# Two TensorE groups moved within the slot of a pipelined attention and feed-forward stack

## The reference

```
def attn_layer(x, Wqkv, qs, ksc, Wo):
    q, k, v = split(x @ Wqkv)                  # 16 heads of 64
    q = l2norm(q) * qs ;  k = l2norm(k) * ksc
    q = q * cos * scale + rotate_half(q) * sin * scale
    k = k * cos / scale + rotate_half(k) * sin / scale
    out = local_attention(q, k, v)             # windows of 32, each sees itself and the one before
    return out @ Wo

def ffn_layer(x, g, bln, W1, b1, W2, b2):
    xn = (x - mean) / sqrt(var + 1e-5) * g + bln
    a, gate = split(xn @ W1 + b1)
    return a * gelu(gate) @ W2 + b2

for i in range(6):
    x = attn_layer(shift_tokens(x), ...) + x
    x = ffn_layer(shift_tokens(x), ...) + x
```

## Time and profile before

| | |
|---|---|
| median of 3 runs | 4420.13 us (4412.47 to 4425.89) |
| the profiled execution | 4411.89 us |
| its span, first to last instruction | 4410.1 us |
| mean granted TensorE clock | 0.966 of full speed |
| TensorE busy | 93% of the span |
| VectorE, ScalarE, GpSimd busy | 79%, 70%, 41% |
| first and last Q projection of the first stack | 393.3 and 2174.8 us |
| first and last Q projection of the second stack | 2553.7 and 4335.5 us |

### The profile page before, as it was taken

One profiled execution on the slowest core, in us unless ns is written; L12 is line 12 of the kernel. 1 busy time (PEld: TensorE's weight loads), 2 busy tenths in 40 slices (PEclk: granted clock), 3 DMA queues, 4 the chain that ended last, 5 costly groups with the idle time before them and its releaser, 6 DMA issues. The chain is left out here.

```text
span 4410.1 us, 111762 instructions
## 1 busy us (share of the span) xinstructions
PE 4119.1 (93%) x43089; PEld 2408.1 (55%) x43089; DVE 3484.4 (79%) x4981; ACT 3076.0 (70%) x7032; POOL 1802.7 (41%) x1071
## 2 busy tenths in 40 slices
PE   7997999999999999999967589999999999999998
PEld 3443555555555555555536445555555555555554
DVE  5775888888888888888735478888888888888886
ACT  3555777777777777777762267777777777777776
POOL 3112444444444444444404534444444444444442
PEclk7999999999999999999986699999999999999999
DMA  2213444444443444444300044434434444444342
GB/s 43 30 21 80 100 107 97 102 103 94 106 107 84 109 103 99 101 103 99 74 10 3 3 119 102 106 90 110 105 87 108 101 104 94 100 102 106 90 97 54
DMA packets 232516, 380.72 MB, mean 86 GB/s; under 512 B 59364, under 2 KB 122336, under 8 KB 231688
## 3 DMA queue, kind: packets, MB, share of 16 engines
q1 hardware_dynamic: 231560, 372.20, 36.3%
q10 hardware_dynamic: 384, 0.79, 0.1%
HBM read 39.22 MB, written 1.05 MB: 9 GB/s over the span
## 5 line engine op out<-in xcount | busy, mean ns | idle before, releaser
L835 POOL TENSOR_TENSOR b_prob<-b_prob,b_rinv 128x768 f32<-128x768 f32 x384 | 564.9, 1471 | 1857.9 <-DVE b_rinv L1262 1857.9
L841 POOL TENSOR_TENSOR b_prc<-b_prc,b_sws 128x1024 f32<-128x1024 f32 x384 | 910.8, 2372 | 64.3 <-DMA b_sws<-b_prs 64.1
L1130 ACT ACTIVATE b_prob<-ps,b_nmx 128x96 f32<-128x96 f32 x3072 | 751.2, 363 | 0.0
L879 PEld LDWEIGHTS ps<-ident,b_prob 128*128 128x128 f32 x3072 | 377.5, 141 | 421.7 <-issue 302.4
L1203 DVE SCALAR_TENSOR_TENSOR b_prc<-ps,b_qks,b_rot 128x512 f32<-128x512 f32 x768 | 571.2, 744 | 10.6 <-ACT b_sq L1091 10.2
L1205 DVE SCALAR_TENSOR_TENSOR b_prs<-ps,b_qks,b_rot 128x512 f32<-128x512 f32 x768 | 570.3, 743 | 0.0
L1243 DVE TENSOR_TENSOR b_prc<-b_prc,ps 128x512 f32<-128x512 f32 x384 | 264.2, 688 | 381.7 <-PE ps L937 307.4
L1216 DVE SCALAR_TENSOR_TENSOR b_rsp<-b_rhi,b_minus_hi,b_rn 128x512 fp32r<-128x512 f32 x192 | 412.3, 2147 | 110.6 <-ACT b_rn L1077 110.6
L879 PE MATMUL ps<-ident,b_prob 128*128 128x128 f32 x3072 | 464.8, 274 | 5.3 <-ACT b_pT L1066 5.3
L1111 ACT ACTIVATE b_oT<-ps 128x512 f32<-128x512 f32 x384 | 227.0, 591 | 341.9 <-PE ps L895 341.9
L1066 ACT ACTIVATE b_pT<-ps 128x512 f32<-128x512 f32 x724 | 435.6, 602 | 15.1 <-PE ps L879 10.9
(11 more groups left out here) (292 smaller groups left out, 7295.7 us busy)
## 6 DMA issues: line engine op xcount, KB each, us to landing
b_sws<-b_prs SPq DMA_DIRECT2D x1536, 128.0 KB, 2.3
b_vs<-b_va SPq DMA_DIRECT2D x384, 256.0 KB, 3.8
b_wqkv<-in_L_ffn_Wqkv SPq DMA_DIRECT2D x96, 192.0 KB, 3.6
b_xs<-y SPq DMA_DIRECT2D x126, 128.0 KB, 2.5
b_wo<-in_L_ffn_Wo SPq DMA_DIRECT2D x96, 64.0 KB, 3.1
b_xs<-y SPq DMA_DIRECT2D x42, 127.8 KB, 2.3
b_rot<-in_rot SPq DMA_DIRECT2D x2, 2048.0 KB, 7.8
b_w<-in_L_ffn_W SPq DMA_DIRECT2D x24, 170.5 KB
```

What stands on the lines that cost most here:

```text
L835: pool.tensor_tensor(prob[:, r, :, P - KEYS:P], prob[:, r, :, P - KEYS:P], rinv[:, r % 2, :].rearrange("p (b a) -> p b a", a=1).broadcast_ ...
L841: pool.tensor_tensor(prc[:, r, :, :], prc[:, r, :, :], sws[:, r % 2, :, :], ALU.add)\
L879: t = pe.transpose(bank[6][:, i * P:(i + 1) * P], prob[:, kd, 4 * e + 2 * h + m, :], ident[:, :])
L1130: g = act.activation(prob[:, kb, i, P - KEYS:P], wide[0][:, e * CH + m * KEYS:e * CH + (m + 1) * KEYS], ACT.Exp, bias=nmx[:, kb % 2, i:i + 1])
```

## The change

Only the order of TensorE's instructions in a slot changes, and only where `before` is not 5 (14 of 16 slots). The two spreads now stand directly behind the Q projection, and the first turn behind them. The second turn stands between the two mask products, not ahead of them. No instruction is added or removed, no semaphore wait is new; each wait goes along with its group. In the slots where `before` is 5 the order stays.

```
+                def mask(kb, e, pe=pe):
+                    pe.matmul(wide[0][:, e * CH:e * CH + 4 * KEYS], identb[:, :], band[:, 1 if kb % 2 else 0, :],
+                              start=True, stop=False, skip_group_check=True)
...
                     if d:
                         UD, kd = um(d)
+                    if d and before == 5:
                         turn(UD, kd, 0)
                     if b:
...
                         pe.matmul(bank[3][:, :], take[:, 2 * (kb % 2) + 1, :], rsp[:, :], start=True, stop=True)\
                             .then_inc(S["nb_mm"], 1)
+                    if d and before != 5:
+                        turn(UD, kd, 0)
                     key_bank_free(f0)
                     if a:
                         pe.wait_ge(S["pk_done"], ONE + U)
                         pe.matmul(bank[1][:, :], W[:, 1, :], X, start=True, stop=True).then_inc(S["k_mm"], 1)
-                    if d:
+                    if d and before == 5:
                         turn(UD, kd, 1)
                     if b:
                         pe.wait_ge(S["exp_done"], ONE + UB)
-                        for e in range(2):
-                            if e:
-                                pe.wait_ge(S["kn_done"], ONE + UB + 1)
-                            pe.matmul(wide[0][:, e * CH:e * CH + 4 * KEYS], identb[:, :], band[:, 1 if kb % 2 else 0, :],
-                                      start=True, stop=False, skip_group_check=True)
+                        mask(kb, 0)
+                    if d and before != 5:
+                        turn(UD, kd, 1)
+                    if b:
+                        pe.wait_ge(S["kn_done"], ONE + UB + 1)
+                        mask(kb, 1)
```

## The result

The changed kernel takes 4385.4 us (median of 7 runs, 4379.9 to 4401.2) beside 4422.5 us for the kernel before (median of 7 runs, 4412.5 to 4431.1). The ratio is 0.9927, with a 95% interval of 0.9909 to 0.9945: faster by 0.7%, 24 to 40 us.

The account below looks back on a forecast made before the run. TensorE, 93% busy, was taken as nearly saturated in the stacks, with only stalls to win: 22 x 6 x 0.16 = 21.1 us less, 4399.0 us against the median; own range 4390 to 4406, all cases 4383 to 4422.

Parts of the forecast that it names:

- The wait of 0.16 us in slots 6 to 8 and 12 to 14: TensorE's second mask product waits for VectorE's k by norms; the reorder was to win 0.16 us in each such slot.
- the sum: 22 half layers x 6 slots x 0.16 us = 21.1 us won; all other slots taken as nothing.
- The pT copy in time for the second turn: ScalarE's copy lets TensorE answer at 1112.17, weights wanted from 1112.18: wait just covered, 0.01 us to spare, cost nothing.
- The bound of 0.1 us for a late load: Most the second turn's wait could cost on TensorE if weights are not loaded ahead: 0.1 us; taken as nothing.
- rival 2: Gain eaten by a late second turn (0.1 us) and 0.20 us lost in slots 5 and 11: 4421, half 4410; chance 0.26.
- Slots 5 and 11 at nothing: Exp between pT copy and Square of k holds the strips at 1083.11 against 1083.13: gain zero; without overlap, 0.20 us lost.
- Slots 0 to 4 as a whole at nothing: The VectorE and GpSimd chain sets these slots, so the first turn's exposed 0.44 us on TensorE changes nothing.
- does not pass through the turn: Claim that the VectorE and GpSimd chain from q by norms to y add avoids the turn; slots 0 to 4 unchanged.
- Slots 9, 10 and 15 at nothing: Slot 10 ends in a wait on a chain begun in slot 9; slots 9 and 15 keep their order: nothing.
- The two first half layers, taken as nothing: First 16 slots of each stack, without feed-forward work, are paced like slots 1 and 2: no change.
- Rival 1: VectorE's split comes ahead of GpSimd's add more often, turning over their port lock: 32 x 0.57 = 18 us, 4381; chance 0.07.

Follow-up runs that it names:

- the control: The changed kernel once more without an edit, beside the kernel before: 4390.9 us (median of 6), ratio 0.9924.

## Why the prediction was right, and where its sizes were off

- **The wait of 0.16 us in slots 6 to 8 and 12 to 14.** Right: 0.162 to 0.167 us in each of the six, 21.6 us over 22 half layers against the 21.1 of the sum.
- **Both parts needed?** The prediction didn't price them apart. My expectations did, and the first was wrong: the spreads alone win 0.12, the turn alone nothing, the pair 0.16.
- **The pT copy in time for the second turn.** Right: its weights come as the first mask product starts. The bound of 0.1 us for a late load was too wide; the experiment with the spreads alone measured 0.05. One leg of rival 2 rested on that price, the other on a loss of 0.20 us in slots 5 and 11 that did not come.
- **Slots 5 and 11 at nothing.** Nearly: 0.027 and 0.042 us less. The sum gave the strips at 1083.11 - 1079.49 = 3.62 us into the slot, and there they stand. The Exp is shown to be the cause.
- **Slots 0 to 4 as a whole at nothing.** Half right. Slot 0 got longer and slot 1 shorter, and undoing the first turn's move in slots 0 and 2 shifts time between neighbours and leaves the sum. But the five together fell by 0.34 us a half layer, 7.6 us in all (0.31 in the control, 0.17 with the spreads alone, none with the turn alone). The step that failed is "does not pass through the turn". The chain passes through the K spread, and the K spread stood behind the first turn on TensorE: where the y add is early, the turn was on the path. A slot 4 of the kernel before, which begins at 1313.14, and the same one of the changed kernel, which begins at 1321.04, show it:

```profile
1312.32 0.69 DVE L1222 TENSOR_TENSOR y<-ps,y 128x512 f32<-128x512 f32 x1
...
1314.67 0.39 PE L937 MATMUL ps<-b_rsp,b_take 128*128 128x512 f32 x1
...
1315.17 0.69 DVE L1243 TENSOR_TENSOR b_prc<-b_prc,ps 128x512 f32<-128x512 f32 x1 [1.14 <-PE ps L937]
```

```profile
1322.13 0.39 PE L942 MATMUL ps<-b_rsp,b_take 128*128 128x512 f32 x1
...
1322.63 0.69 DVE L1251 TENSOR_TENSOR b_prc<-b_prc,ps 128x512 f32<-128x512 f32 x1 [0.71 <-PE ps L942]
```

  The y add is over before the slot begins, VectorE waits 1.14 us, and q by norms starts 2.03 us into the slot; in the changed kernel it starts at 1.59. That is so in 7 of the 22 slots 4; in the others the y add or VectorE's own work comes later. From the start of the half layer, q by norms comes 0.14 us earlier in slot 3, 0.34 in slot 4, and slot 5 begins 0.34 us earlier: so 0.2 us of the 0.34 enter here, and 0.2 in the control and with the spreads alone too. With the first turn back ahead in slots 0 and 2, slot 5 still begins 0.29 us earlier than in the kernel before. What comes before slot 4 differs between executions (0.11 us in the control, none with the spreads alone), and its cause is open. No experiment moved the turn in slot 4 alone, so this rests on the traces.
- **Slots 9, 10 and 15 at nothing.** Slots 9 and 10 fell by 0.09 us together, 2 us in all. It is the same step: in slot 10 of the kernel before, the K spread ends 1.92 us into the slot and q by norms starts 0.11 us after it, at 2.03. Now the K spread ends at 1.48, and q by norms starts at 2.00, when VectorE's preceding instruction lets it. With the 0.04 us by which slot 9 got shorter, that is 0.08 us sooner. In slot 9 itself, whose order stays, q by norms starts at 2.20 and not 2.28 us, and GpSimd's add of slot 8, for which it also waits, ends at 1.97 and not 2.25. Both are readings of the traces.
- **The sum.** 21.6 (as forecast) + 7.6 (slots 0 to 4) + 1.5 (5 and 11) + 2 (9 and 10) - 0.9 (slot 15) = 31.8 us; the medians say 37, their interval 24 to 40, and at equal granted clock it is 32 to 33. The two first half layers, taken as nothing, were 3.3 us longer together in this execution and 5.3 in the control; but they were 3.4 longer with the turn alone too, whose total did not move, so nothing is ascribed to them.
- **Rival 1, the lock.** Its number, 4381, is the nearest to the median, by chance: it did not happen. With splits of 0.74 to 0.85 us in 14 of 192 places in either kernel, the change did not turn over the order. But the mechanism is real, and put to use it brings 10 us (by the slots) to 14 us (by the medians) beyond the change, and 16 to 18 without it.

## What to carry to other kernels

When an engine waits for a result, move its producer up first, and put other work into the wait only then: here the filler alone was worth nothing, since what stood behind it was still waiting. What is lost on an engine in front of a chain that it doesn't set is given back at that chain's next wait, so read slot by slot which chain that is before pricing an exposed instruction. The order of one engine reaches into a chain of other engines wherever a member of that chain stands in its queue, as the K spread does here: ask which link the moved group stands ahead of. And a removed wait shows the next one: look at what stands between the moved instruction and its consumers on the other queues (here an Exp, worth 0.14 us in 44 slots, free to move).

## What the runs showed of the hardware

A weight load of 0.14 us that started 0.02 us ahead of its transposition, and not 0.16 us as in the changed kernel, cost TensorE 0.05 us. A VectorE instruction with two SBUF inputs, of 0.74 to 0.83 us, takes until 0.54 us after the end of a GpSimd addition if it starts 0.11 us behind it, and makes the addition longer (2.82 us in place of 2.35) if it starts 0.20 us ahead of it; one edit of its place made it short in 23 of 24 slots.
